# Graph attention on TensorE: four rows at a time instead of two, with three banks for transposed rows and one for the v product

## The chip, the cores and the metric

The kernel runs on one core of a Trainium2 chip. The metric is the device time of one execution in microseconds (us).

## What is computed

Four layers work on the same 512 nodes with 512 features and on 8704 edges, each with a residual and a layer norm around it: dense attention with a bias made of the edges (layer 0), a graph convolution (1), a relational convolution with a two-layer product behind it (2), and attention along the edges with a two-layer product (3). The change touches the two attentions alone. Layer 0, cut to it:

```python
bias = full((n, n), NEG); bias[diag, diag] = 0.0; bias[dst, src] = edge_weight
q, k, v = split(x @ Wqkv.T + bqkv, 3)            # 8 heads of 64 features
scores = einsum('hnd,hmd->hnm', q, k) / sqrt(64) + bias
attn = softmax(scores, axis=-1)
out = einsum('hnm,hmd->hnd', attn, v)            # then out @ Wo.T + bo
h = layer_norm(x + attn_out, g1, beta1)
```

Layer 3 has the same sum over the edges of a node, which the kernel also computes densely: the bias is then the logarithm of how often an edge occurs, and the rows with no edge are set to zero by a factor (`deg`).

## The kernel before

Everything is written for one core with a program of its own for each engine. The order on each engine is written out by hand, and semaphores carry what one needs of another: `full[b]` and `free[b]` count the uses of PSUM bank b. `psum_plan` gives each tile its bank and its number among the bank's uses; `begin(name)` on TensorE waits until the use before it was freed, `finish` says that the tile is full, `frees` that it was read.

The program runs: counts of the edges (two sweeps), q, k and v of layer 0, attention 0, output projection, layers 1 and 2, v, q and k of layer 3, attention 3 (so called after its layer), output projection, and the last product.

An attention has 32 **rows** (the code's items m): a row is one block of 128 nodes of one head, against all 512. Eight rows in a row belong to one pair of heads p, four blocks i times two heads e. Each row goes through the engines like this:

- TensorE, L600: the **scores**, a 128x512 tile in bank m % 4. Three products (the high and low halves of q and k) of 64 partitions each; the two heads of a pair stand on different halves of the partitions, so two rows are computed side by side.
- VectorE, L1272 (`peak_of`): scale, bias and row maximum in one instruction, out of the bank into `sp` (a ring of six, two of whose tiles are called `rel_rows` and `deg_rows`). This frees the bank.
- ScalarE, L830: the exponent, with its sum. VectorE, L1279: the sum's reciprocal. POOL, L381 (`scale_rows`): the row is scaled; after every third row POOL also makes the low half of a later weight piece (L367).
- TensorE, L609: four **transposes** into one bank for `probT`, 4 + m % 2. ScalarE (L838, even rows) or VectorE (L1295, odd rows) copies them to `probT` in SBUF, which has room for four heads.
- TensorE, L625: the **v product** of a pair of heads into one bank (6 + p % 2), in four **quarters** j, each of two instructions with two passes. When it is complete, ScalarE (L800) writes its high half to `th` and VectorE (L1048) its low half to `tl` and frees the bank; this pair of copies is `mixed`.

On TensorE a step q is: scores of rows 2q and 2q + 1, transposes of rows 2q - 4 and 2q - 3, and from step 6 on one quarter. The last pair's four quarters come in one step at the end. In attention 0 VectorE also has `call_sum(0)` (L1247 to L1252), which sums four planes of edge counts for the next layer; it comes behind the copies of the last rows and ahead of the low halves of the third and fourth pair. TensorE's program behind attention 0 is the output projection, whose first instruction is L478 (attention 3: L507).

```python
for t in (2 * q - 4, 2 * q - 3):
    if 0 <= t < ITEMS:
        pe.wait_ge(s["scaled"], base + t + 1)
        begin(("probT", a, t))
```

Of the kernel before, what the change touches and what calls it, by code (L numbers as in the profile page):

```python
# [26 lines left out]
P = 128  # L27
# [37 lines left out]
def psum_plan():  # L65
# [7 lines left out]
    def attention(a):  # L73
        for m in range(ITEMS):
            use(("score", a, m), m % 4)
            use(("probT", a, m), 4 + m % 2)
        for p in range(HEADS // 2):
            use(("mix", a, p), 6 + p % 2)
# [41 lines left out]
PAIR = 2 * T  # L120

# [12 lines left out]
def build(nc, x0, x0t, edges, edge_rows, edge_w, weights, rows_of, cols_of, rel_b, ident_d, iota_d, later_d, out):  # L134
# [5 lines left out]
    with ExitStack() as ctx:  # L140
# [119 lines left out]
        def ps(name):  # L260
            return bank[PLAN[name][0]]
# [202 lines left out]
        def _(pe):  # L464
# [123 lines left out]
            def attention(a, base):  # L588
# [3 lines left out]
                for q in range(ITEMS // 2 + 5):  # L592
                    if q < ITEMS // 2:
# [10 lines left out]
                    for t in (2 * q - 4, 2 * q - 3):  # L604
# [6 lines left out]
                    last = HEADS // 2 - 1  # L611
                    quarters = [(p, j) for p in range(last) for j in range(T) if q == 4 * p + 6 + j]
                    if q == 4 * last + 6:
                        quarters = [(last, j) for j in range(T)]
                    for p, j in quarters:
                        name = ("mix", a, p)
                        if j == 0:
                            wait_freed(pe, ("probT", a, PAIR * p + PAIR - 2))
                            wait_freed(pe, ("probT", a, PAIR * p + PAIR - 1))
# [171 lines left out]
        def _(act):  # L791
# [33 lines left out]
            def attention(a, base):  # L825
                for m in range(ITEMS + 4):
                    if m < ITEMS:
                        wait_freed(act, ("score", a, m))
                        c = base + m
                        act.activation(sp[m % SP][:], sp[m % SP][:], ACT.Exp, bias=peak[:, c:c + 1], scale=-1.0,  # L830
                                       accum_out=total[:, c:c + 1]).then_inc(s["exped"], 1)
                    t = m - 4
                    if t >= 0 and t % 2 == 0:
                        p, i, e, hd = item(t)
                        if hd >= 4:
                            wait_full(act, ("mix", a, p - 2))
                        wait_full(act, ("probT", a, t))
                        frees(act.copy(probT[:, hd % 4, :, i * P:(i + 1) * P],  # L838
                                       ps(("probT", a, t))[:].rearrange("p (j n) -> p j n", j=T)), ("probT", a, t))
                    if m >= 20 and (m - 20) % PAIR == 0:  # L840
                        mixed(a, (m - 20) // PAIR)
# [757 lines left out]
```

## Time and profile before

| what | us |
|---|---|
| median of 3 runs | 569.53 (568.75 to 570.74) |
| the profiled execution's own time | 569.0 |
| its span | 566.1 |
| TensorE busy | 524.4 |
| VectorE busy | 395.6 |
| POOL busy | 268.2 |
| ScalarE busy | 225.9 |

The span is from the first to the last instruction on the core; the 2.9 us between it and the execution's own time lie around the program. In the profile PE is TensorE, PEld its weight loads, DVE VectorE, ACT ScalarE, SP SyncE; L12 is line 12 of the kernel. The ends of matmuls are modelled, so their starts are the better measure. A float32 transpose or quarter shows as one instruction for each pass.

### The profile page before, as it was taken

How to read it: one execution, taken by the hardware profiler on the slowest of the kernel's cores; microseconds unless marked ns; L12 is line 12 of the kernel's file. 1: busy time of each engine (PE TensorE's matmuls, PEld its weight loads, DVE VectorE, ACT ScalarE, POOL GpSimd, SP SyncE). 2: the span in 40 equal slices, each digit the busy share in tenths (PEclk: the TensorE clock that was granted, in tenths of full speed). 3: DMA queues.
4: the chain of work that ended last, by engine and by line, in shares of the span. 5: the costliest groups of instructions: out<-in, count | busy, mean ns of one | idle time of the engine just before them, and what ended most of it. 6: DMA issues, size and time to landing. Idle time of an engine off the chain costs nothing.

```text
span 566.1 us, 7808 instructions
## 1 busy us (share of the span) xinstructions
PE 524.4 (93%) x2540; PEld 348.7 (62%) x2540; DVE 395.6 (70%) x946; ACT 225.9 (40%) x473; POOL 268.2 (47%) x258
## 2 busy tenths in 40 slices
PE   7399999999998999998999999998999998999881
PEld 2144444444875554776777888887877885554760
DVE  6988898999986777766666863546327635774647
ACT  2030080003526665557441233234624225765435
POOL 5546645667828776003540561443242653766000
PEclk9699999999999999999999999999999999999997
DMA  6950000000177220233653553212462853100001
GB/s 207 379 205 0 2 0 1 0 0 2 38 260 231 67 56 19 47 122 113 187 149 109 150 167 105 100 41 72 125 178 70 259 169 83 48 2 1 0 0 75
DMA packets 30169, 54.37 MB, mean 96 GB/s; under 512 B 4962, under 2 KB 6446, under 8 KB 29624
## 3 DMA queue, kind: packets, MB, share of 16 engines
q1 hardware_dynamic: 17212, 29.50, 17.1%
q0 software_dynamic: 11696, 18.91, 11.5%
q10 hardware_dynamic: 1228, 5.54, 2.6%
q8 instruction: 17, 0.28, 0.2%
q14 instruction: 16, 0.13, 0.1%
HBM read 51.78 MB, written 2.17 MB: 95 GB/s over the span
## 4 chain that ended last, share of the span: by engine, by line
PE 72%; DVE 9%; POOL 5%; DMA 5%; ACT 4%; issue 4%; SPq 0%; DVEq 0%; POOLq 0%; ACTq 0%
PE bank L530 18%; PE bank L507 10%; PE bank L509 9%; PE bank L508 9%; PE bank L625 5%; PE bank L609 4%; PE bank L600 3%; PE bank L702 3%; PE bank L704 3%; PE bank L703 3%; POOL edge_bias L409 2%; POOL wl L367 2%; DVE ewn L1160 2%; DMA wraw<-w_o 1%; PE bank L577 1%
## 5 line engine op out<-in xcount | busy, mean ns | idle before, releaser
L367 POOL TENSOR_TENSOR wl<-wraw,wh 128x512 fp32r<-128x512 f32 (+1 forms) x78 | 104.1, 1352 | 94.1 <-DMA wh<-w 15.4
L530 PE MATMUL bank<-hot 128*128 128x512 bf16 x544 | 119.6, 383 | 10.5 <-DVE hot L1136 10.5
L530 PEld LDWEIGHTS bank<-hot 128*128 128x128 bf16 x544 | 53.4, 99 | 76.7 <-DVE hot L1136 11.9
L409 POOL DMA_INDIRECT edge_bias<-ewn,cell_at x68 | 76.5, 1125 | 45.0 <-DVE cell_at L1130 24.3
L507 PE MATMUL bank<-wh,tl 128*128 128x512 f32 x176 | 70.9, 403 | 1.1 <-POOL wl L367 1.0
L509 PE MATMUL bank<-wh,th 128*128 128x512 f32 x176 | 68.8, 391 | 0.0
L508 PE MATMUL bank<-wl,th 128*128 128x512 f32 x176 | 68.8, 391 | 0.0
L830 ACT ACTIVATE sp<-sp,peak 128x512 f32<-128x512 f32 x44 | 31.8, 722 | 24.8 <-DVE peak L1272 24.4
L1136 DVE TENSOR_SCALAR hot<-iota,pair_dst,digit 128x1024 bf16<-128x1024 f16 x68 | 41.0, 602 | 0.0
L1118 DVE SCALAR_TENSOR_TENSOR eq<-keyb,key,later 128x384 f16<-128x384 f16 (+1 forms) x68 | 40.7, 623 | 0.0
L507 PEld LDWEIGHTS bank<-wh,tl 128*128 128x128 f32 x176 | 33.0, 188 | 12.3 <-issue 4.2
L1272 DVE CUSTOM_DVE_ANT_0 sp<-bank,nbias 128x512 f32<-128x512 f32 x44 | 29.8, 684 | 11.2 <-PE bank L600 11.2
L509 PEld LDWEIGHTS bank<-wh,th 128*128 128x128 f32 x176 | 33.0, 188 | 7.2
L508 PEld LDWEIGHTS bank<-wl,th 128*128 128x128 f32 x176 | 33.1, 188 | 6.3
L1135 DVE TENSOR_SCALAR hot<-iota,ef 128x512 bf16<-128x512 f16 x68 | 26.7, 392 | 12.9 <-PE bank L530 11.3
L625 PE MATMUL bank<-probT,v 128*64 128x512 f32 x128 | 33.0, 612 | 0.0
L1048 DVE TENSOR_TENSOR tl<-bank,th 128x512 fp32r<-128x512 f32 x32 | 21.9, 687 | 15.5 <-ACT th L805 9.8
L507 PE MATMUL bank<-th,wl 128*128 128x512 f32 x80 | 31.2, 390 | 0.9 <-issue 0.9
L508 PE MATMUL bank<-tl,wh 128*128 128x512 f32 x80 | 31.1, 389 | 0.0
L509 PE MATMUL bank<-th,wh 128*128 128x512 f32 x80 | 31.1, 389 | 0.0
L815 ACT ACTIVATE gap<-h,neg 128x512 f32<-128x512 f32 x24 | 17.4, 725 | 28.3 <-DVE neg L1059 28.3
L800 ACT CAST msgh<-bank 128x512 fp32r<-128x512 f32 x16 | 9.4, 588 | 42.9 <-DVE bank L1372 42.9
(202 smaller groups left out, 1072.3 us busy)
## 6 DMA issues: line engine op xcount, KB each, us to landing
wraw<-w SPq DMA_DIRECT2D x26, 256.0 KB, 2.7
wh<-w POOLq DMA_DIRECT2D x6, 1024.0 KB, 6.0
keyb<-edge_keys ACTq DMA_DIRECT2D x4, 1088.0 KB, 11.9
wh<-w_rel POOLq DMA_DIRECT2D x4, 1024.0 KB, 6.3
wraw<-w_rel SPq DMA_DIRECT2D x16, 256.0 KB, 2.8
wraw<-w_qkv SPq DMA_DIRECT2D x8, 256.0 KB, 6.3
wh<-w_o POOLq DMA_DIRECT2D x2, 1024.0 KB, 5.9
wraw<-w_o SPq DMA_DIRECT2D x8, 256.0 KB, 3.7
```

The costliest lines, as they stand in the source:

```text
L367: pool.tensor_tensor(wl[n % WSLOTS][:, k, 0:width], wraw[:, q % 3, 0:width], wh[n % WSLOTS][:, k, 0:width], ALU.subtract).then_inc(s["w_lo ...
L409: pool.indirect_dma_start(out=bias_dram, out_offset=bass.IndirectOffsetOnAxis(ap=cell_at[:, c:c + 1], axis=0), in_=ewn[:, c:c + 1], in_off ...
L507: pe.matmul(ps(name)[:], al, bh, start=start and k == 0, stop=False)
L508: pe.matmul(ps(name)[:], ah, bl, start=False, stop=False)
L509: mm = pe.matmul(ps(name)[:], ah, bh, start=False, stop=stop and k == ks - 1)
L530: mm = pe.matmul(ps(name)[:], hot[:, slot, 0, i * P:(i + 1) * P], hot[:, slot, 1 + kind, :], start=False, stop=last, skip_group_check=True)
L625: mm = pe.matmul(ps(name)[HD * e:HD * e + HD, :], v[:, j, hd * HD:(hd + 1) * HD], probT[:, hd % 4, j, :], start=j == 0, stop=j == T - 1, s ...
L830: act.activation(sp[m % SP][:], sp[m % SP][:], ACT.Exp, bias=peak[:, c:c + 1], scale=-1.0, accum_out=total[:, c:c + 1]).then_inc(s["exped" ...
L1118: return dve.scalar_tensor_tensor(out=eq[:, k, :], in0=keyb[:, bass.ds(c * P, WINDOW * P)], scalar=key[:, bass.ds(c, 1)], in1=later[:], op ...
L1135: dve.tensor_scalar(hot[:, slot, 0, :], iota[:, 0:N], ef[:, 0, bass.ds(j, 1)], None, ALU.is_equal)
L1136: dve.tensor_scalar(hot[:, slot, 1:3, :].rearrange("p a n -> p (a n)"), iota[:], pair_dst[:, bass.ds(j, 1)], digit[:, bass.ds(j, 1)], ALU. ...
L1272: frees(dve.tensor_tensor_reduce(sp[m % SP][:], ps(name)[:], nbias[:, item(m)[1], :], -HD ** -0.5, 3e38, ALU.add, ALU.min, peak[:, c:c + 1 ...
```

## The change

One step of TensorE is now a **batch** b of four rows: scores of rows 4b to 4b + 3, transposes of rows 4b - 4 to 4b - 1, and from batch 3 on two quarters. Transposed rows go round three banks (4, 5, 6), and all four v products use bank 7. ScalarE and VectorE get orders to match: copies of transposed rows lie between exponents and between peaks, and `mixed` of the first two pairs stands at the start of batches 5 and 7. `call_sum(0)` stays where it was.

```diff
--- before.py
+++ after.py
@@ -73,9 +73,9 @@
     def attention(a):
         for m in range(ITEMS):
             use(("score", a, m), m % 4)
-            use(("probT", a, m), 4 + m % 2)
+            use(("probT", a, m), 4 + m % 3)
         for p in range(HEADS // 2):
-            use(("mix", a, p), 6 + p % 2)
+            use(("mix", a, p), 7)
 
     def tiles(name, first, n=4):
         for i in range(n):
@@ -118,6 +118,7 @@
 PLAN = psum_plan()
 
 PAIR = 2 * T
+BATCHES = ITEMS // 4
 
 
 def item(m):
@@ -589,8 +590,10 @@
                 q_done, k_done, v_done = 4 * (a // 3 + 1), 4 * (a // 3 + 1), 4 * (a // 3 + 1)
                 pe.wait_ge(s["q_ready"], q_done)
                 pe.wait_ge(s["k_ready"], k_done)
-                for q in range(ITEMS // 2 + 5):
-                    if q < ITEMS // 2:
+                for b in range(BATCHES + 2):
+                    for q in (2 * b, 2 * b + 1):
+                        if q >= ITEMS // 2:
+                            break
                         for part, (left, right) in enumerate(((ql, kh), (qh, kl), (qh, kh))):
                             for m in (2 * q, 2 * q + 1):
                                 p, i, e, hd = item(m)
@@ -601,22 +604,19 @@
                                                start=part == 0, stop=part == 2)
                                 if part == 2:
                                     finish(mm, ("score", a, m))
-                    for t in (2 * q - 4, 2 * q - 3):
+                    for t in range(4 * b - 4, 4 * b):
                         if 0 <= t < ITEMS:
                             pe.wait_ge(s["scaled"], base + t + 1)
                             begin(("probT", a, t))
                             for j in range(T):
                                 mm = pe.transpose(ps(("probT", a, t))[:, j * P:(j + 1) * P], sp[t % SP][:, j * P:(j + 1) * P], ident[:])
                             finish(mm, ("probT", a, t))
-                    last = HEADS // 2 - 1
-                    quarters = [(p, j) for p in range(last) for j in range(T) if q == 4 * p + 6 + j]
-                    if q == 4 * last + 6:
-                        quarters = [(last, j) for j in range(T)]
+                    quarters = [(p, j) for p in range(HEADS // 2) for j in range(T) if min(2 * p + 3 + j // 2, BATCHES + 1) == b]
                     for p, j in quarters:
                         name = ("mix", a, p)
                         if j == 0:
-                            wait_freed(pe, ("probT", a, PAIR * p + PAIR - 2))
-                            wait_freed(pe, ("probT", a, PAIR * p + PAIR - 1))
+                            for t in range(PAIR * p + PAIR - 3, PAIR * p + PAIR):
+                                wait_freed(pe, ("probT", a, t))
                             if p == 0:
                                 pe.wait_ge(s["v_ready"], v_done)
                             begin(name)
@@ -823,25 +823,38 @@
                 act.wait_ge(normed[L], i + 1)
 
             def attention(a, base):
-                for m in range(ITEMS + 4):
-                    if m < ITEMS:
-                        wait_freed(act, ("score", a, m))
-                        c = base + m
-                        act.activation(sp[m % SP][:], sp[m % SP][:], ACT.Exp, bias=peak[:, c:c + 1], scale=-1.0,
-                                       accum_out=total[:, c:c + 1]).then_inc(s["exped"], 1)
-                    t = m - 4
-                    if t >= 0 and t % 2 == 0:
-                        p, i, e, hd = item(t)
-                        if hd >= 4:
-                            wait_full(act, ("mix", a, p - 2))
-                        wait_full(act, ("probT", a, t))
-                        frees(act.copy(probT[:, hd % 4, :, i * P:(i + 1) * P],
-                                       ps(("probT", a, t))[:].rearrange("p (j n) -> p j n", j=T)), ("probT", a, t))
-                    if m >= 20 and (m - 20) % PAIR == 0:
-                        mixed(a, (m - 20) // PAIR)
-                for p in range(HEADS // 2):
-                    if PAIR * p + 20 >= ITEMS + 4:
-                        mixed(a, p)
+                def exponent(m):
+
+                    wait_freed(act, ("score", a, m))
+                    c = base + m
+                    act.activation(sp[m % SP][:], sp[m % SP][:], ACT.Exp, bias=peak[:, c:c + 1], scale=-1.0,
+                                   accum_out=total[:, c:c + 1]).then_inc(s["exped"], 1)
+
+                def even_row(t):
+
+                    p, i, e, hd = item(t)
+                    if hd >= 4:
+                        wait_full(act, ("mix", a, p - 2))
+                    wait_full(act, ("probT", a, t))
+                    frees(act.copy(probT[:, hd % 4, :, i * P:(i + 1) * P],
+                                   ps(("probT", a, t))[:].rearrange("p (j n) -> p j n", j=T)), ("probT", a, t))
+
+                for b in range(BATCHES + 1):
+                    if b >= 5 and b % 2:
+                        mixed(a, (b - 5) // 2)
+                    if b < BATCHES:
+                        exponent(4 * b)
+                    if b:
+                        even_row(4 * b - 4)
+                    if b < BATCHES:
+                        exponent(4 * b + 1)
+                    if b:
+                        even_row(4 * b - 2)
+                    if b < BATCHES:
+                        exponent(4 * b + 2)
+                        exponent(4 * b + 3)
+                for p in range(2, HEADS // 2):
+                    mixed(a, p)
 
             def mixed(a, p):
                 high(("mix", a, p), th[:, p, :], s["th_ready"])
@@ -1278,29 +1291,38 @@
                     dve.wait_ge(s["exped"], c + 1)
                     dve.reciprocal(scale[:, c:c + 1], total[:, c:c + 1]).then_inc(s["inverse"], 1)
 
-                for q in range(ITEMS // 2 + 2):
-                    if q < ITEMS // 2:
-                        peak_of(2 * q)
-                    if 1 <= q <= ITEMS // 2:
-                        inverse_of(2 * q - 2)
-                        inverse_of(2 * q - 1)
-                    if q < ITEMS // 2:
-                        peak_of(2 * q + 1)
-                    t = 2 * q - 3
-                    if t >= 0:
-                        p, i, e, hd = item(t)
-                        if hd >= 4:
-                            wait_full(dve, ("mix", a, p - 2))
-                        wait_full(dve, ("probT", a, t))
-                        frees(dve.tensor_copy(probT[:, hd % 4, :, i * P:(i + 1) * P],
-                                              ps(("probT", a, t))[:].rearrange("p (j n) -> p j n", j=T)), ("probT", a, t))
-                    if q >= 11 and (q - 11) % T == 0:
-                        mixed(a, (q - 11) // T)
+                def odd_row(t):
+
+                    p, i, e, hd = item(t)
+                    if hd >= 4:
+                        wait_full(dve, ("mix", a, p - 2))
+                    wait_full(dve, ("probT", a, t))
+                    frees(dve.tensor_copy(probT[:, hd % 4, :, i * P:(i + 1) * P],
+                                          ps(("probT", a, t))[:].rearrange("p (j n) -> p j n", j=T)), ("probT", a, t))
+
+                for b in range(BATCHES + 1):
+                    if b:
+                        inverse_of(4 * b - 1)
+                    if b < BATCHES:
+                        peak_of(4 * b)
+                        if b >= 5 and b % 2:
+                            mixed(a, (b - 5) // 2)
+                        peak_of(4 * b + 1)
+                    if b:
+                        odd_row(4 * b - 3)
+                    if b < BATCHES:
+                        inverse_of(4 * b)
+                        peak_of(4 * b + 2)
+                        inverse_of(4 * b + 1)
+                    if b:
+                        odd_row(4 * b - 1)
+                    if b < BATCHES:
+                        peak_of(4 * b + 3)
+                        inverse_of(4 * b + 2)
                 if a == 0:
                     call_sum(0)
-                for p in range(HEADS // 2):
-                    if T * p + 11 > ITEMS // 2 + 1:
-                        mixed(a, p)
+                for p in range(2, HEADS // 2):
+                    mixed(a, p)
 
             def mixed(a, p):
                 base = 0 if a == 0 else 24
```

The end of attention 0 on TensorE before, from the last transposed rows on (`free4` and so on are the waits for bank 4; L625 are the quarters, the last row is the output projection):

```order
L625 MATMUL bank<-probT,v 64x512 x2
L609 MATMUL bank<-ident,sp 128x128 [waits free4,scaled]
L609 MATMUL bank<-ident,sp 128x128 x3
L609 MATMUL bank<-ident,sp 128x128 [waits free5,scaled]
L609 MATMUL bank<-ident,sp 128x128 x3
L625 MATMUL bank<-probT,v 64x512 x2
L625 MATMUL bank<-probT,v 64x512 [waits free7,free5,free4]
L625 MATMUL bank<-probT,v 64x512 x7
L478 MATMUL bank<-add,ones 128x512 [waits free0,w_low,add2_ready]
```

The same place in the changed kernel:

```order
L612 MATMUL bank<-ident,sp 128x128 [waits free4,scaled]
L612 MATMUL bank<-ident,sp 128x128 x3
L612 MATMUL bank<-ident,sp 128x128 [waits free5,scaled]
L612 MATMUL bank<-ident,sp 128x128 x3
L625 MATMUL bank<-probT,v 64x512 x4
L625 MATMUL bank<-probT,v 64x512 [waits free5,free7,free4,free6]
L625 MATMUL bank<-probT,v 64x512 x7
L479 MATMUL bank<-add,ones 128x512 [waits free0,w_low,add2_ready]
```

Two quarters of the third pair now come after the last transposes instead of one, and the `free7` of the last pair stands for the use of bank 7 by the third pair, which before was in bank 6.

VectorE in the changed kernel over the same stretch (L1300 copies a transposed row, L1260 to L1265 are `call_sum`, L1061 the low halves of the third and fourth pair):

```order
L1300 COPY probT<-bank 128x4x128 [waits full4,full7]
L1285 ISA sp,peak<-bank,nbias 128x512 [waits full5,full3]
L1285 ISA peak 128x1
L1292 RECIPROCAL scale<-total 128x1 [waits exped] x2
L1300 COPY probT<-bank 128x4x128 [waits full6,full7]
...
L1260 TENSOR_TENSOR call_a<-counts 128x1024
L1261 TENSOR_TENSOR call_a<-call_a,counts 128x1024 [waits dve_chain]
L1262 TENSOR_TENSOR call_a<-call_a,counts 128x1024 [waits dve_chain]
L1265 TENSOR_TENSOR call_a<-call_a,ident 128x128 [waits dve_chain]
L1061 TENSOR_TENSOR tl<-bank,th 128x512 [waits th_ready] x2
```

The last five operations stand in the same order as before; what is new is that TensorE's last quarters wait for the first of the two in the last row.

## Rows read from the trace of the kernel before

**Rows 1.** The page: busy time of each engine, and the chain that ended last.

```profile
PE 524.4 (93%) x2540; PEld 348.7 (62%) x2540; DVE 395.6 (70%) x946; ACT 225.9 (40%) x473; POOL 268.2 (47%) x258
...
PE 72%; DVE 9%; POOL 5%; DMA 5%; ACT 4%; issue 4%; SPq 0%; DVEq 0%; POOLq 0%; ACTq 0%
```

**Rows 2.** Windows: length, busy us of PE, PEld, DVE, ACT, POOL, clock, DMA.

```profile
172.90:187.80 14.90, 12.46 (x83) 8.04 (x82) 12.76 (x44) 11.34 (x29) 12.48 (x17) 1.00 0.76 227
187.80:219.00 31.20, 30.92 (x189) 15.94 (x188) 21.56 (x71) 21.41 (x54) 23.22 (x29) 1.00 0.18 52
```

**Rows 3.** Timeline of TensorE in attention 0, middle: start, length, operation.

```profile
189.73 0.66 PE L609 MATMUL bank<-ident,rel_rows 128*128 128x128 f32 x4
...
190.75 1.08 PE L625 MATMUL bank<-probT,v 128*64 128x512 f32 x4
191.76 0.50 PE L600 MATMUL bank<-kh,ql 64*128 64x512 f32 x2
...
192.66 1.09 PE L609 MATMUL bank<-ident,sp 128*128 128x128 f32 x8
```

**Rows 4.** Timeline of VectorE and ScalarE, the same stretch.

```profile
193.38 0.22 DVE L1279 RECIPROCAL scale<-total 128x1 f32<-128x1 f32 x2
193.49 0.72 ACT L830 ACTIVATE rel_rows<-rel_rows,peak 128x512 f32<-128x512 f32 x1 [0.92 <-DVE peak L1272]
...
194.12 0.18 ACT L830 ACTIVATION_READ_ACCUMULATOR rel_rows<-rel_rows,peak 128x1 f32 x1
194.22 0.56 ACT L838 COPY probT<-bank 128x512 f32<-128x512 f32 x1
```

**Rows 5.** Timeline, start of attention 0: first scores, peaks, transposes, first quarter.

```profile
172.89 0.50 PE L600 MATMUL bank<-kh,ql 64*128 64x512 f32 x2
...
173.69 0.55 PE L600 MATMUL bank<-kh,ql 64*128 64x512 f32 x2
...
174.01 0.69 DVE L1272 CUSTOM_DVE_ANT_0 sp<-bank,nbias 128x512 f32<-128x512 f32 x1 [0.32 <-PE bank L600]
...
187.83 1.08 PE L625 MATMUL bank<-probT,v 128*64 128x512 f32 x4
```

**Rows 6.** Timeline, end of attention 0, TensorE and VectorE.

```profile
218.99 4.62 PE L625 MATMUL bank<-probT,v 128*64 128x512 f32 x20
219.17 0.69 DVE L1295 COPY probT<-bank 128x512 f32<-128x512 f32 x1 [1.34 <-PE bank L609]
219.78 1.20 DVE L1247 TENSOR_TENSOR call_a<-counts 128x1024 int16<-128x1024 int16 x1
...
223.54 0.50 PE L478 MATMUL bank<-add,ones 2*128 2x512 f32 x1
...
224.77 1.28 DVE L1048 TENSOR_TENSOR tl<-bank,th 128x512 fp32r<-128x512 f32 x2
```

**Rows 7.** Timeline of TensorE, attention 3: first scores, and the projection's first matmul.

```profile
473.22 0.50 PE L600 MATMUL bank<-kh,ql 64*128 64x512 f32 x2 [1.50 <-issue]
...
523.02 0.50 PE L507 MATMUL bank<-wh,tl 128*128 128x512 f32 x1
```

**Rows 8.** TensorE around its idle stretches: timeline, then windows (busy us, instructions, granted clock).

```profile
23.24 1.03 PE L530 MATMUL bank<-hot 128*128 128x512 bf16 x2 [9.28 <-DVE hot L1136]
...
554.18 0.40 PE L509 MATMUL bank<-wh,hidh 128*128 128x512 f32 x1
...
16.00:21.00 5.00, 0.00 (x0) 0.54 0.91 378
...
26.00:31.00 5.00, 5.00 (x23) 0.94 1.01 406
...
556.00:561.00 5.00, 0.00 (x0) 0.81 0.18 69
```

**Rows 9.** Longest waits of TensorE, 223 to 300, then 300 to 400 us: total, times, longest.

```profile
PE bank L671 <- DVE rowl L1346: 2.0, 3, 1.0
...
PE bank L493 <- DVE tl L1048: 1.6, 1, 1.6
```

## The prediction

> **What bounds the kernel now.** I read the page first. TensorE is busy for 93% of the span and carries 72% of the chain that ended last [rows 1], so a microsecond of TensorE delay is a microsecond of kernel unless a later stage absorbs it. Next I read the windows over the two attention stages, the only code the diff touches [rows 2]. Each has three parts. In the start (172.9 to 187.8) TensorE is busy 12.46 of 14.90 us: the ring score, peak, exponent, scale, transpose is being filled. In the middle (187.8 to 219.0) it is busy 30.92 of 31.20 us. In the end it runs quarters of the v product alone. The second attention has the same shape.
>
> Then the timeline of TensorE [rows 3]. One step of the old order is two transposed rows, one quarter and two scores. Transposes begin at 189.73 and again at 192.66, so a step is 2.93 us and four rows 5.86. The transposes take 1.02 of it (to 190.75), the quarter 1.01 (to 191.76), the scores 0.90. Where the kind of work changes the first matmul costs more: the scores of rows 0 and 1 are followed by those of rows 2 and 3 after 0.80 us instead of 0.90 [rows 5]; a row's four transposes last 0.66 and eight last 1.09, so four more inside a run cost 0.43; five quarters in a row take 4.55 us, from 218.99 to 223.54 [rows 6], so each after the first costs (4.55 - 1.01) / 4 = 0.89.
>
> **What the change removes.** No matmul, copy, exponent or DMA goes or comes; only order and banks change. A batch of four rows has one run of each kind where there were two. That saves 0.10 on scores, about 0.15 on transposes (2.04 becomes 1.02 + 2 x 0.43) and 0.12 on quarters: 0.37 us a batch, so the batch takes 0.80 + 0.90 + 1.88 + 1.90 = 5.5 us instead of 5.86. Five batches with quarters save 1.8 us in each attention. The first batches have no quarters, and there TensorE isn't what sets the pace.
>
> **What it adds, one: a ring of 5.2 us a batch.** With three banks for four transposed rows, the fourth row of a batch waits until ScalarE has copied out the first one, and ScalarE does that copy behind the exponent of the next batch's first row. That exponent hangs on VectorE, and this on the fourth row of the batch before. I add the ring up from one fourth row to the next: its transposes 0.66 [rows 3]; VectorE's copy of it 0.61, to the start of the next operation [rows 6]; the peak of the last score 0.69 [rows 5]; its exponent with the sum 0.81; the reciprocal 0.11; the next peak 0.69; the next exponent up to the copy 0.73; ScalarE's copy 0.56 [rows 4]. That is 4.86, and eight handovers at the 0.03 to 0.06 seen between these rows make it 5.2. It is shorter than 5.5, so it hides in the batches with quarters, and longer than the 3.6 us of work in those without.
>
> **The layout of one attention**, from its first score matmul. Old order in the trace [rows 5, 6]: first quarter at 187.83 - 172.89 = 14.9, transposes done at 218.99 - 172.89 = 46.1, end at 223.54 - 172.89 = 50.7. New order: row 3 is transposed at about 7.25. (Rows 4 to 7 must be scored first, and row 7 waits for the peak of row 3. The first peak starts at 174.01; three more, with two reciprocals between them that wait for the exponents, put the end of the fourth at 4.2, the end of row 7's scores at 5.1. Rows 0 to 2 are transposed from 5.1; row 3 waits for the copy of row 0, which stands behind the exponent of row 4.) Two turns of the ring later, at 17.65, row 11 is transposed and at 18.2 the first quarter starts. That is 3.3 later than before, with the work of four more rows done. Four batches at 5.55 (5.5 and a few hundredths of waiting at the fourth row) lead to 40.5. Two quarters, 1.9, and the last four rows, 2.6 with 0.7 of waiting for copies that no scores cover any more, lead to 45.2. **So up to here 0.9 us are won, while one quarter has been put off**: six remain instead of five. The faster batches are nearly eaten by the ring at the start.
>
> **What it adds, two: the bank of the v product.** All four head pairs now use bank 7. The last pair's first quarter waits until VectorE has taken the third pair's low part out of it; before, it waited for the second pair's, long gone. In attention 0 VectorE's program has the sum of the counts ahead of that low part, as the order printed ahead shows. It starts at 219.78 and the low parts at 224.77, so 4.99 us stand ahead [rows 6]. New order: last transposes 45.2, copy of row 31 until 45.9, sum until 50.9, low part 0.65 more, so TensorE may go on at about 51.6. Its two quarters of the third pair were through at 47.1. **It stands for about 4.5 us**, then takes 3.6 for the last four quarters: end at 55.2 instead of 50.7, **4.5 us later**. Queued behind that wait are the output projection and all after it. VectorE's own delay (the last low part now comes after the last quarters, the two low parts of the counts behind it) is as long and lies beside it. POOL's weights and residual are done sooner than needed; their DMAs wait for buffers, not for TensorE's last quarters, and cost nothing.
>
> In attention 3 there is no such sum. The order is the same, from 473.22 to 523.02 in the trace, 49.8 us [rows 7] (its start is faster, since the weight pieces that POOL takes between its scale operations are half as wide there). The new layout is bound by the ring, which has no POOL in it, so it gives 45.2 again. Two quarters end at 47.2, ScalarE's high part, 0.6 like its other copies, and VectorE's low part, 0.65, follow with handovers, TensorE goes on at 48.6 after 1.5 us, and ends at 52.2: **2.4 us later**.
>
> **TensorE's clock.** This trace shows it twice after idleness [rows 8]. TensorE's matmuls end at 13.96, and the mean of 0.54 for 16 to 21 says that the granted clock was at half (1.2 GHz) from about 16.4. Work came back at 23.24 and the clock at 26.6 (0.94 over 26 to 31 is 0.6 us of half), after 3.4 us at half speed. At the end the last matmul ends at 554.6 and the clock falls near 559.1 (0.81 over 556 to 561), 4.5 us later. In between, with no gap over 1.6 us, it stays at 1.00. A gap of some 4 us lies between the falls after 2.4 and after 4.5. Both ends: no fall costs 0, a fall costs half of the 3.4 us until the clock is back, 1.7. I take the fall: the gap at 13.96 also had matmuls without a pause ahead of it, and there it took only 2.4.
> The Trainium skill ("TensorE: Matmul & The Clock Gate", Why this matters for your kernels) also has idle gaps of a few microseconds between bursts throw the engine back to half rate; by that rule the sum is the 577.6 below, without it 575.9.
>
> **Sum.** 4.5 + 2.4 + 1.7 = 8.6 on the profiled execution's 569.0 gives **577.6 us**. That execution is 0.5 below the median of the three runs, 569.53, and inside their spread.
> Between the attentions TensorE's waits are for VectorE and ScalarE, at most 2.0 us in one group from 223 to 300 and 1.6 us from 300 to 400 [rows 9]. Those work on what TensorE hands them and come later with it; no wait there is for POOL or a DMA, which could have stood still meanwhile. So nothing absorbs the delay.
>
> **Rivals.**
> *The clock holds* (chance 0.24). All else as above: 575.9. The fall at the end, after 4.5 us, speaks for it. Still slower.
> *The wait for the bank is covered* (0.04). This is also the case that the order isn't what I read. Then both attentions end as the layout says without the wait: 45.2 + 1.9 + 3.6 = 50.7 against 50.7, and 50.7 against 49.8: 570, no change. For it: nothing; the order shows the sum of the counts ahead of the low part.
> *TensorE alone sets the pace* (0.04). If ScalarE's copy of a batch's first row is done before the fourth row's transposes are due, the ring doesn't close. Then two starts of 5.2 become 3.6 (3.2 saved), and the waits at row 3 and at the last rows go (about 1.4): 4.6 in each attention, 577.6 - 9.2 = 568.4, and with the clock holding 566.7, faster. It decides at 1.3 us after the batch's first transpose; the copy needs its exponent to end by then, and that hangs on a peak that the fourth row before holds up.
> *The ring closes in the full batches too* (0.06). A few handovers of 0.1 instead of 0.04 bring it from 5.2 to over 5.5; at 5.8 all ten full batches cost 0.3 more: 580.6.
> The forecast itself has 0.62.
>
> **How the numbers follow.** A measurement of this kernel can tell about 0.3%, 1.7 us, from no change. The forecast, the clock that holds and the longer ring are slower: 0.92. The covered bank is within: 0.04. TensorE alone: 0.04 faster. The range runs from 1.9 below the clock that holds, 574.0, for errors of the layout (on the old order it comes within 0.2 us of the trace in each attention), to 580.6, the longer ring; beyond both ends lies about 0.15 to 0.2.
>
> **What would show it.** Right: attention 0 lasts 55 us and attention 3 52, first score to first matmul of the output projection; TensorE idle 4 to 5 us before the last pair's quarters in attention 0, 1.5 in attention 3, released by VectorE's low part; granted clock under 1.00 around 220 to 230; waits of 0.7 to 0.8 at the fourth row and at the scores of rows 7, 11 and 15; batches of 5.5 in the middle. Wrong: a middle batch of 5.8 or more, no gap in attention 0, or a later stage that is shorter than before.

## The result and the profile after

| | before | changed |
|---|---|---|
| median of the runs, us | 569.47 (568.75 to 570.74, 4 runs) | 577.66 (576.59 to 578.23, 4 runs) |
| the profiled execution, us | 569.0 | 577.45 |
| its span, us | 566.1 | 575.4 |

The changed kernel takes 1.0143 times as long, interval 1.0123 to 1.0163: slower by 8.2 us. The forecast was 577.6.

The page answers to [rows 1]: no engine's busy time rose by as much as 1% (the weight loads beside TensorE's matmuls by just 1%), TensorE's busy share fell, and VectorE's share of the chain rose from 9% to 11%. The third row is new in the waits: the v product, released by VectorE's low part.

```profile
PE 524.7 (91%) x2525; PEld 352.3 (61%) x2540; DVE 398.2 (69%) x946; ACT 227.0 (39%) x473; POOL 269.0 (47%) x258
...
PE 70%; DVE 11%; DMA 5%; ACT 5%; POOL 4%; issue 4%; SPq 0%; DVEq 0%; POOLq 0%; ACTq 0%
...
L625 PE MATMUL bank<-probT,v 128*64 128x512 f32 x128 | 31.9, 626 | 6.6 <-DVE tl L1061 6.6
```

The windows over attention 0, with the columns of [rows 2]: start, middle, and the end from 219.00 on, just after the third pair's last two quarters began.

```profile
173.80:192.10 18.30, 15.52 (x97) 9.93 (x96) 14.55 (x49) 13.05 (x34) 15.22 (x19) 1.00 0.62 188
192.10:219.00 26.90, 26.51 (x171) 15.38 (x172) 20.15 (x66) 20.43 (x50) 20.11 (x26) 1.00 0.20 58
219.00:230.60 11.60, 6.55 (x24) 1.84 (x20) 6.46 (x7) 0.59 (x1) 4.88 (x4) 0.85 0.00 0
```

The start is 3.4 longer, the middle 4.3 shorter, and the end, which was 4.55 us of quarters, is 11.6 us long. The timeline of TensorE shows the pieces (start, length, operation, idle time before it and its releaser): the first scores, the wait at the fourth row, one that has POOL in it, one batch of the middle (from score to score), the third and fourth row of another, and the end.

```profile
173.80 0.50 PE L603 MATMUL bank<-kh,ql 64*128 64x512 f32 x2
...
181.07 0.63 PE L612 MATMUL bank<-ident,sp 128*128 128x128 f32 x4 [0.64 <-ACT probT L839]
...
191.54 0.66 PE L612 MATMUL bank<-ident,deg_rows 128*128 128x128 f32 x4 [0.70 <-POOL deg_rows L382]
192.12 1.94 PE L625 MATMUL bank<-probT,v 128*64 128x512 f32 x8
193.99 0.50 PE L603 MATMUL bank<-kh,ql 64*128 64x512 f32 x2
...
199.59 0.50 PE L603 MATMUL bank<-kh,ql 64*128 64x512 f32 x2
...
207.72 0.60 PE L612 MATMUL bank<-ident,rel_rows 128*128 128x128 f32 x4
208.37 0.63 PE L612 MATMUL bank<-ident,deg_rows 128*128 128x128 f32 x4
...
218.72 1.94 PE L625 MATMUL bank<-probT,v 128*64 128x512 f32 x8
...
225.71 5.00 PE L625 MATMUL bank<-probT,v 128*64 128x512 f32 x16 [5.05 <-DVE tl L1061]
230.63 0.50 PE L479 MATMUL bank<-add,ones 2*128 2x512 f32 x1
```

POOL in that start, ahead of the scale of row 5: a weight piece that waited for its DMA:

```profile
183.03 1.28 POOL L368 TENSOR_TENSOR wl<-wraw,wh 128x512 fp32r<-128x512 f32 x1 [1.36 <-DMA wh<-w]
```

VectorE beside the end, the counterpart of [rows 6]: the sum of the counts, which starts behind its last transposed row, and only then the low part that frees bank 7.

```profile
219.51 1.58 DVE L1260 TENSOR_TENSOR call_a<-counts 128x1024 int16<-128x1024 int16 x1
...
220.71 0.59 ACT L800 CAST th<-bank 128x512 fp32r<-128x512 f32 x1 [2.11 <-PE bank L625]
...
224.47 0.49 DVE L1265 TENSOR_TENSOR call_a<-call_a,ident 128x128 int16<-128x128 int16 x2
224.88 0.69 DVE L1061 TENSOR_TENSOR tl<-bank,th 128x512 fp32r<-128x512 f32 x1
```

ScalarE has the high part written at 221.3; the low part could follow at once, and starts at 224.88. The clock meanwhile, in windows of TensorE (length, busy us, instructions, granted clock, DMA):

```profile
221.00:226.00 5.00, 0.29 (x2) 0.90 0.00 0
226.00:231.00 5.00, 5.00 (x17) 0.75 0.00 0
```

0.90 over 5 us is 1.0 us at half speed (1.2 GHz), 0.75 is 2.5: the clock was low from about 225.0 to 228.5. The sixteen passes of the last quarters took 4.92 us, from 225.71 to 230.63.

Attention 3, the counterpart of [rows 7]: three fourth rows 5.13 apart, the last of all transposed rows, the wait of 1.50 before the last pair, and the projection.

```profile
480.48 0.50 PE L603 MATMUL bank<-kh,ql 64*128 64x512 f32 x2 [1.51 <-issue]
...
487.71 0.63 PE L612 MATMUL bank<-ident,sp 128*128 128x128 f32 x4 [0.63 <-ACT probT L839]
...
492.84 0.63 PE L612 MATMUL bank<-ident,sp 128*128 128x128 f32 x4 [0.69 <-ACT probT L839]
...
497.97 0.63 PE L612 MATMUL bank<-ident,deg_rows 128*128 128x128 f32 x4 [0.70 <-ACT probT L839]
...
524.62 0.66 PE L612 MATMUL bank<-ident,sp 128*128 128x128 f32 x4 [0.29 <-POOL sp L382]
...
528.65 3.65 PE L625 MATMUL bank<-probT,v 128*64 128x512 f32 x16 [1.50 <-DVE tl L1061]
532.23 0.50 PE L508 MATMUL bank<-wh,tl 128*128 128x512 f32 x1
```

So attention 0 lasts 56.83 us, first score to first matmul of the projection (50.65 before), and attention 3 lasts 51.75 (49.80). These 6.2 and 1.95 are the 8.2 between the medians. The spans lie 9.3 apart; 0.9 of that is ahead of attention 0, in code that is the same, and its start moves from 172.99 to 174.34 between the profiles of the kernels below. Between the attentions 249.85 us pass, 0.2 more than before, so nothing was absorbed there.

All experiments start from the changed kernel. "Length" below is measured as here.

### The profile page after: what moved, and what is told of

It is laid out like the page before. It is cut to its first block, busy times and chain, and to the rows that moved or that the text cites. A ratio compares the mean times of both kernels' runs of the same rounds, so it can differ in the third digit from the quotient of the medians.

```text
span 575.4 us, 7799 instructions
## 1 busy us (share of the span) xinstructions
PE 524.7 (91%) x2525; PEld 352.3 (61%) x2540; DVE 398.2 (69%) x946; ACT 227.0 (39%) x473; POOL 269.0 (47%) x258
## 4 chain that ended last, share of the span: by engine, by line
PE 70%; DVE 11%; DMA 5%; ACT 5%; POOL 4%; issue 4%; SPq 0%; DVEq 0%; POOLq 0%; ACTq 0%
PE bank L531 18%; PE bank L508 10%; PE bank L510 9%; PE bank L509 9%; PE bank L625 4%; PE bank L612 3%; PE bank L702 3%; PE bank L704 3%; PE bank L703 3%; PE bank L603 2%; POOL edge_bias L410 2%; DVE ewn L1173 2%; DMA wraw<-w_o 1%; PE bank L578 1%; DMA wh<-w 1%
## 5 line engine op out<-in xcount | busy, mean ns | idle before, releaser
L410 POOL DMA_INDIRECT edge_bias<-ewn,cell_at x68 | 77.7, 1142 | 43.9 <-DVE cell_at L1143 25.4
L1061 DVE TENSOR_TENSOR tl<-bank,th 128x512 fp32r<-128x512 f32 x32 | 22.0, 688 | 23.8 <-ACT th L800 13.7
L625 PE MATMUL bank<-probT,v 128*64 128x512 f32 x128 | 31.9, 626 | 6.6 <-DVE tl L1061 6.6
L612 PE MATMUL bank<-ident,sp 128*128 128x128 f32 x176 | 24.8, 278 | 2.8 <-ACT probT L839 2.0
```

The costliest lines, as they stand in the source:

```text
L410: pool.indirect_dma_start(out=bias_dram, out_offset=bass.IndirectOffsetOnAxis(ap=cell_at[:, c:c + 1], axis=0), in_=ewn[:, c:c + 1], in_off ...
L612: mm = pe.transpose(ps(("probT", a, t))[:, j * P:(j + 1) * P], sp[t % SP][:, j * P:(j + 1) * P], ident[:])
L625: mm = pe.matmul(ps(name)[HD * e:HD * e + HD, :], v[:, j, hd * HD:(hd + 1) * HD], probT[:, hd % 4, j, :], start=j == 0, stop=j == T - 1, s ...
```

## Experiments: the wait before the last pair

**e1_sum_behind.** The sum of the counts steps behind the low part of the third pair. The shared bank stays.

```diff
+                mixed(a, 2)
                 if a == 0:
                     call_sum(0)
-                for p in range(2, HEADS // 2):
-                    mixed(a, p)
+                mixed(a, 3)
```

> The changed kernel with one thing moved: on VectorE the sum of the counts (4.99 us) goes behind the third pair's low part instead of ahead of it. Theory of the prediction: TensorE's wait in attention 0 falls from 5.05 us to about 1.5, as in attention 3, that is 3.5 us less, of which 0.4 may come back through the last low part; with so short a gap the granted clock stays at full, 1.4 us more: 577.7 - 4.7 = about 573. Rival, the clock has nothing to do with it: about 574.5, and the clock still falls near 225. Rival, the batches themselves cost and VectorE's work only moves its wait to the next stage: not below 576.5.

Measured: 571.69 (5 runs), 1.0048 of the kernel before, interval 1.003 to 1.0066. Timeline of POOL, VectorE and TensorE at the end of attention 0:

```profile
217.49 4.94 POOL L391 TENSOR_TENSOR y<-x,par 128x512 f32<-128x512 f32 x4
...
220.77 0.69 DVE L1061 TENSOR_TENSOR tl<-bank,th 128x512 fp32r<-128x512 f32 x1 [1.74 <-ACT th L800]
221.38 1.61 DVE L1260 TENSOR_TENSOR call_a<-counts 128x1024 int16<-128x1024 int16 x1
...
223.02 0.69 DVE L1261 TENSOR_TENSOR call_a<-call_a,counts 128x1024 int16<-128x1024 int16 x1
223.74 0.69 DVE L1262 TENSOR_TENSOR call_a<-call_a,counts 128x1024 int16<-128x1024 int16 x1
...
221.61 3.65 PE L625 MATMUL bank<-probT,v 128*64 128x512 f32 x16 [1.50 <-DVE tl L1061]
...
225.19 0.50 PE L479 MATMUL bank<-add,ones 2*128 2x512 f32 x1
```

The wait is 1.50 instead of 5.05, as in attention 3, where there never was a sum. The quarters take 3.58 instead of 4.92 at a granted clock of 1.00. Attention 0 is 51.68 long: one line moved on VectorE brings 5.15 of the 6.2 us back. That is 3.55 of waiting, 1.34 of clock, and 0.2 of the start, which had no wait for POOL in this execution. The median fell by 6.0 where 4.7 was expected; the expectation had 3.5 for the wait, less 0.4 that did not come back, and 1.4 for the clock, and attention 0 also began 0.3 sooner here. The rivals are out: the clock did not fall, and the time is below 574.5. Attention 3, which the edit doesn't touch, stays at 51.76.

**e2_busy_gap** keeps the wait and keeps TensorE busy in it. In attention 0 eighteen products of q and k are added ahead of the last pair, written to bank 0, which the output projection overwrites.

```diff
+                            if a == 0 and p == 3:
+                                begin(("o0", 0))
+                                for n in range(18):
+                                    pe.matmul(ps(("o0", 0))[:], qh[:, 0, 0:P], kh[:, 0, :], start=True, stop=True)
```

> The changed kernel with 18 extra matmuls of 0.22 us (4 us of TensorE work) in the gap ahead of the last pair's quarters of attention 0, into a bank that is free; their results are overwritten. The wait for the bank stays, only TensorE is no longer idle in it. Theory: the clock holds, the four quarters take 3.6 us instead of 4.9, the time falls by 1.4 us to 576.3. Rival, a fall of the clock that costs nothing, since VectorE sets the pace behind: 577.7. Rival, the extra matmuls delay the quarters: above 577.7.

Measured: 575.91 (4 runs), 1.0126, interval 1.0104 to 1.0149. Timeline and then windows of TensorE:

```profile
219.93 4.38 PE L625 MATMUL bank<-kh,qh 128*128 128x512 f32 x18
225.02 3.65 PE L629 MATMUL bank<-probT,v 128*64 128x512 f32 x16 [0.71 <-DVE tl L1065]
228.60 0.50 PE L479 MATMUL bank<-add,ones 2*128 2x512 f32 x1
...
226.00:231.00 5.00, 5.00 (x24) 1.00 0.00 0
```

The quarters start when they did (51.6 us after the first score; 51.9 in the changed kernel, whose start was 0.2 longer), but at full clock, and take 3.58. So the wait costs 3.55 by itself (5.05 less 1.50) and the clock 1.34 on top. The intervals of the ratios of the changed kernel and of this one overlap; the quarters' length in the trace is the evidence, the 1.75 us between the medians only agree with it.

**e8_half_gap** is the same edit with `range(9)`, for an idle stretch of a length in between.

> As e2, with 9 extra matmuls instead of 18: 2 us of work, then about 2.9 us without any ahead of the last pair's quarters of attention 0. Theory that every gap of a few microseconds brings the clock down: the quarters take 4.9 us or more again and the time is that of the changed kernel, 577.7. Rival, a gap of this length is short enough: quarters 3.6 us, 576 as in e2. The first fall that a profile showed came 2.4 us after the last matmul, the wait of 1.5 us in attention 3 never brought one; 2.9 lies between the two kinds, so I put it at even odds.

Measured: 577.28 (575.99 to 578.14, 4 runs), 1.0137, interval 1.0096 to 1.0177. Timeline and a window of TensorE:

```profile
225.93 3.65 PE L629 MATMUL bank<-probT,v 128*64 128x512 f32 x16 [2.70 <-DVE tl L1065]
...
226.00:231.00 5.00, 5.00 (x22) 1.00 0.00 0
```

In the profiled execution 2.70 us idle brought no fall. The other runs reach up to what a fall would give, and no profile of them exists. The profiled execution takes 0.9 more than that of e2 because attention 0 starts at 174.34 instead of 173.42, and not by its quarters. Whether the clock fell in some of the other runs stays open: this run tells the two apart only for the execution that was profiled.

## Experiments: the banks and the ring

**e3_two_v_banks** gives the third bank back: two banks for transposed rows, two for the v product, with the order of the change.

```diff
-            use(("probT", a, m), 4 + m % 3)
+            use(("probT", a, m), 4 + m % 2)
...
-            use(("mix", a, p), 7)
+            use(("mix", a, p), 6 + p % 2)
```

> The new order with the old banks: two for transposed rows, two for the v product. Theory, by the same layout: no wait ahead of the last pair's quarters in either attention, but the third row of each batch now waits for the copy of the first (about 1.2 us in the first batches, 0.6 in the middle ones), so a middle batch takes 5.9 us and each attention 53.4: 569.5 + 2.7 + 3.6 = 575.8. Rival, the single bank for the v product is the whole cost and the batches gain: 566.5.

Measured: 575.54 (4 runs), 1.0109, interval 1.0081 to 1.0137. The waits of TensorE in attention 0 (total, times, longest), and one batch of the middle:

```profile
PE bank L612 <- ACT probT L839: 5.3, 7, 1.1
```

```profile
194.27 0.50 PE L603 MATMUL bank<-kh,ql 64*128 64x512 f32 x2
...
197.42 1.06 PE L612 MATMUL bank<-ident,sp 128*128 128x128 f32 x8 [0.48 <-ACT probT L839]
...
200.28 0.50 PE L603 MATMUL bank<-kh,ql 64*128 64x512 f32 x2
```

Both attentions last 53.4, as expected. The wait for bank 7 is gone, and the third row of each batch now waits for ScalarE: a batch takes 6.01, longer than the 5.86 of four rows in the old order. So the two halves of the change belong together: a run of four transposes over two banks is worse than two runs of two. Against the changed kernel this gains in attention 0 (56.83 to 53.4) and loses in attention 3 (51.75 to 53.4). The bank trade alone is worth 1.6 us where no sum stands in the way.

**e5_copy_first** aims at the ring. ScalarE's copy of a batch's first row goes ahead of the exponent of the next one.

```diff
+                    if b:
+                        even_row(4 * b - 4)
                     if b < BATCHES:
                         exponent(4 * b)
-                    if b:
-                        even_row(4 * b - 4)
```

> The changed kernel with one swap on ScalarE: the copy of a batch's first transposed row ahead of the exponent of the next batch's first row. Theory of the ring: its path through that exponent is cut, but the exponent now waits for the transposes, and the fourth score waits longer in its place; by the layout the first batches get only 0.2 to 0.7 us shorter in each attention: about 577. Rival, the wait at the fourth row is the whole loss of the start (0.7 us in each of three batches) and goes without a price: 577.7 - 4.2 = 573.5.

Measured: 576.14 (7 runs), 1.0109, interval 1.0075 to 1.0143. The first quarter of attention 3 comes after 17.28 instead of 18.05, so 0.8 is won in three turns. The waits of TensorE in attention 3 tell why not more:

```profile
PE bank L603 <- DVE peak L1285: 1.9, 4, 0.8
```

That was 0.9 in the changed kernel. The later exponent delays what hangs on it, and the ring seems to close over the peaks. Attention 3 is 50.94 long, 0.8 shorter. Attention 0 is 57.20, longer by 0.4, though its first quarter too comes 0.6 sooner. The time is nearer to the 577 expected than to the rival's 573.5. Timeline and windows of TensorE:

```profile
225.29 5.95 PE L625 MATMUL bank<-probT,v 128*64 128x512 f32 x16 [5.05 <-DVE tl L1061]
231.18 0.50 PE L479 MATMUL bank<-add,ones 2*128 2x512 f32 x1
...
221.00:226.00 5.00, 0.71 (x2) 0.71 0.00 0
226.00:231.00 5.00, 5.00 (x16) 0.60 0.00 0
```

The same idle stretch of 5.05 us, and 2.9 + 4.0 us at half speed instead of 3.5: the quarters take 5.89.

**e6_pairs_at_start** does the first twelve rows in the old steps of two and goes over to batches at row 12, with ScalarE and VectorE to match (core of the edit, TensorE):

```diff
-                for b in range(BATCHES + 2):
+                for q in range(6):
+                    scores((q,))
+                    turned_rows((2 * q - 4, 2 * q - 3))
+                for b in range(3, BATCHES + 2):
```

> The changed kernel with the first twelve scored and eight transposed rows in steps of two, as before the change, on all engines; batches of four from the first quarter on. Banks, sum of the counts and end as in the change. Theory: the start no longer goes at the ring's 5.2 us a batch; by the layout attention 0 gets 0.8 us shorter and attention 3 1.5: 575.4. Rival, the ring at the start costs nothing against the old steps: 577.7.

Measured: 576.27 (574.33 to 578.05, 9 runs), 1.0107, interval 1.0079 to 1.0136. First quarter of attention 3 after 16.67, transposes done at 43.3 instead of 44.7, length 50.36. Attention 0 is 55.82. Its end again has a fall, here 1.9 + 1.5 us long:

```profile
224.47 5.16 PE L636 MATMUL bank<-probT,v 128*64 128x512 f32 x16 [5.05 <-DVE tl L1076]
229.56 0.49 PE L479 MATMUL bank<-add,ones 2*128 2x512 f32 x1
...
221.00:226.00 5.00, 1.53 (x4) 0.81 0.00 0
226.00:231.00 5.00, 5.00 (x19) 0.85 0.00 0
```

Starting in pairs is worth 1.4 us in attention 3 and 1.0 in attention 0 (1.5 and 0.8 were expected), the latter although its quarters took 0.17 more at the low clock. The edit takes away the ring and the longer first batches together; how much of the 1.4 is the ring alone is not shown.

## Experiments: a version that keeps the batches

**e4_quarters_first** leaves banks and sum and moves the third pair's last two quarters ahead of the last four transposes, with `mixed(a, 2)` early on ScalarE and VectorE (core, TensorE):

```diff
+                    for part in ((quarters_of, rows_turned) if b == BATCHES else (rows_turned, quarters_of)):
+                        part(b)
```

> The changed kernel with, in both attentions, the third pair's last two quarters ahead of the last four transposed rows, its high and low part taken out ahead of those rows' copies, and the sum of the counts behind that low part. Theory: nothing waits for bank 7 any more, 0.9 us stay for the copy of the last row; each attention takes 50.7: 569.5 + 0.0 + 0.9 = 570.4. Rival, the loss is in the batches and not in the bank's wait: above 574.

Measured: 570.24 (10 runs), 1.0016, interval 1.0003 to 1.0029. Timeline of TensorE at the end of attention 0:

```profile
220.30 3.65 PE L630 MATMUL bank<-probT,v 128*64 128x512 f32 x16 [1.05 <-DVE probT L1309]
```

By the interval it is still slower than the kernel before, by about 0.8 us. The copies out of bank 7 now lie beside the last transposes. What is left is 1.05 us for the copy of row 31. Both attentions last 50.8: even in attention 0, and 1.0 behind the old order in attention 3.

**e7_pairs_and_quarters_first** is e6's start with e4's end.

> The start of e6 and the end of e4 together: steps of two until the first quarter, batches of four in the middle, the third pair's quarters ahead of the last transposed rows, the sum of the counts behind its low part. Theory: what is left is the gain of the middle, 0.37 us a batch: by the layout 49.9 us for attention 0 and 49.2 for attention 3, against 50.65 and 49.8 before the change: 568.2. Rival, the batches gain nothing even in the middle: 570 or more.

Measured: 567.78 (566.05 to 571.01, 12 runs) beside 569.61 (25 runs) of the kernel before: 0.9965, interval 0.9939 to 0.9992. It beats both kernels, by 1.8 us with an interval that ends near zero. Attention 3 is 49.37, 0.4 shorter than before. Attention 0 is 50.72 in the profile, no shorter. VectorE at its start tells why:

```profile
173.68 1.53 DVE L1295 TENSOR_TENSOR v<-bank,par 128x512 f32<-128x512 f32 x2 [0.15 <-DVE v L1295]
175.49 0.69 DVE L1308 CUSTOM_DVE_ANT_0 sp<-bank,nbias 128x512 f32<-128x512 f32 x1 [0.27 <-DVE v L1295]
```

In this execution VectorE still had two copies of v to make when the first scores were done, and its first peak came 2.10 us after the first score (at 173.39). Before it was 1.12 [rows 5]. In e6, whose start has the same order, it was 1.12 too, and the first quarter came 17.17 after the first score; here it came after 18.03. So this start cost about 0.9, and without it attention 0 would be 49.9, as expected. That the other executions had no such start is inferred, no profile of them exists. The two profiled executions have equal spans (566.1 before, 566.2 here), so the gain of 1.8 stands on the medians alone.

## Why the prediction was right

The time, 577.66 for 577.6, and the steps:

- **The batch.** 5.5, or 5.55 with the wait at the fourth row, was forecast; it measured 5.60 (193.99 to 199.59). Its scores took 1.60 (forecast 1.70), its transposes 2.13 (195.59 to 197.72; forecast 1.88), its quarters 1.87 (1.90), so the transposes are the term that was too small. The fourth row starts 0.65 after the third (207.72 to 208.37) instead of 0.43, and 0.14 after ScalarE's copy of the batch's first row has ended (at 208.23). So a wait of about 0.2 for that copy is left in the full batches, where a few hundredths were forecast. A batch saves 0.26 of 5.86, where the term was 0.37 with no wait in it. Direction right, size two thirds.
- **The ring.** 5.2 forecast, 5.13 measured in attention 3, with waits of 0.63 to 0.70 for ScalarE's copy. Row 3 came 7.27 after the first score (forecast 7.25), the first quarter 18.3 and 18.05 (18.2). Adding the ring up out of single rows and handovers worked. The waits at the scores of rows 7, 11 and 15 were 0.2 to 0.3, not the 0.7 to 0.8 that was named as a sign.
- **POOL in the ring** was not forecast. In attention 0 of this profile two rows wait for POOL's scale, the longer time 0.70 (the row at 191.54), and the first quarter is 0.3 later than in attention 3. It belongs to this execution and not to the order: POOL's weight piece at 183.03, ahead of the first of these scales, had waited for its DMA and began 9.2 us after the first score. In e1, e2, e4 and e8, whose start has the same order, it began after 7.8 to 8.5, no row of the start waits for POOL, and the first quarter comes after 18.1.
- **Transposes done** at 45.2 forecast, 44.9 and 44.7 measured (the starts of the quarters behind them). The faster batches were eaten by the start, as the layout said: 1.2 and 0.5 us are left of them, with one quarter put off. The layout's own terms, 40.5 and 1.9 and 2.6, add up to 45.0; the 45.2 is 0.2 more than they give.
- **The bank of the v product, attention 0.** The gap of 5.05 is released by the low part, with all four planes of the sum ahead of it, as the order of VectorE said it would be. TensorE went on at 51.9 (forecast 51.6): the sum took 5.37 us (219.51 to 224.88) where the layout had the 4.99 of [rows 6]; the whole difference is its first operation, 1.58 instead of 1.20. Without the clock's share, attention 0 is 4.85 longer (4.5 forecast). e1 shows the cause: with the sum behind the low part the wait is 1.50.
- **Attention 3.** 1.50 us of waiting as forecast, length 51.75 instead of 52.2: 1.95 longer than before instead of 2.4. Of the 0.45 too much, 0.2 is the adding named above, and about 0.2 lies in the last four rows: they took 2.41 instead of 2.6, and the one wait there is the 0.29 for POOL at 524.62, not 0.7 for ScalarE's copies.
- **The clock.** The fall came, between the two ends: 4.4 us after the last matmul's end at 220.66, beside 2.4 and 4.5 in [rows 8]. It cost 1.34, the forecast was 1.7. The term took half of the 3.4 us that the clock stayed low in [rows 8] after work came back. Here that was 2.8 us (225.71 to 228.5), half of it 1.4. The same works for e5 (4.7 us, 2.3 lost) and e6 (3.0 us, 1.5 lost), so this time differs from profile to profile, and the forecast could not know which one it would meet.
The Trainium skill ("TensorE: Matmul & The Clock Gate", Why this matters for your kernels) has idle gaps of a few microseconds throw the engine back; the trace agrees for all three profiles with a gap of 5.05, and the 2.70 of e8 brought no fall.
- **Nothing absorbs it.** The same groups of waits stand behind attention 0 as in [rows 9], and the stretch between the attentions kept its length.

The mechanism was right in each large term, and the closeness of the number was in part luck. The misses are 0.35 too little and 0.45 too much for the two attentions, and 0.35 too much for the clock. They cancel in part: the three terms measured 8.15 for 8.6. The 0.45 that is left is hidden by the base, the profiled execution's 569.0, which lies 0.5 below the median of the runs; that is how the median came within 0.1 us. A fall like that of e5 would have added 1 us.

The rivals: the clock that holds is refuted in this profile, the covered bank by the wait of 5.05, TensorE alone by the waits at the fourth row. The ring that closes in the full batches too, at 5.8 a batch, is refuted by the 5.60, though a wait of 0.2 is left there.

## What to carry to other kernels

When buffers are traded between two uses, ask for the one that loses a buffer where the instruction that frees it stands in its engine's queue. One unrelated sum of 5 us ahead of it cost more than all the faster batches gave; its move alone brought 5 us back.

Longer runs of one kind saved a tenth of a microsecond per change of kind, but they lengthened the pipeline's start and put work off to its end. Short steps at the start, long ones in the middle and the buffer's last use pulled forward at the end shed most of the price: e7 came out 1.8 us ahead of the kernel before, with an interval from 0.5 to 3.5.

## What the runs showed of the hardware

- **The same idle stretch, different falls.** Three profiles had TensorE idle for 5.05 us at the same place. The clock fell about 4.4 (changed kernel), 2.9 (e5) and 4.7 us (e6) after the last matmul and stayed at half for about 3.5, 6.9 and 3.4 us; the quarters behind it took 4.92, 5.89 and 5.09 us instead of 3.58. An edit can look up to 1 us worse (e5, attention 0) through this alone. Stretches of 2.70 (e8), 1.50 (e1), 1.05 (e4) and 0.71 us (e2) ahead of the same quarters showed no fall in their profiles.
- **POOL beside VectorE doubles the time of the sum.** In e1 POOL's four operations of L391 end at 222.43. The operation of the sum that starts before that takes 1.61, the two that start behind it 0.69 each. In the changed kernel L391 runs until 223.9, and all three operations of the sum over the planes take about 1.6. e4 shows the same border: L391 ends at 222.5, the operation that starts at 221.39 takes 1.64, the one at 223.06 takes 0.69. The first one, beside POOL in all profiles, varies from 1.1 (e3) to 1.6. So of the 5.37 us that stood ahead of the low part, about 2.7 (three operations, 0.9 each) come from POOL's work beside it. That is an estimate from the rows of e1; no kernel without that work of POOL's was run. The Trainium skill ("SBUF — State Buffer", Who interferes with whom) has a VectorE instruction with two inputs in SBUF contend with a GpSimd instruction that reads SBUF; these rows agree.
- **A start varies by a microsecond.** Code that no edit touches put the start of attention 0 between 172.99 and 174.34 us in the profiles of the changed kernels, and VectorE's first peak came 1.12 us behind the first score in all profiles but that of e7, where it was 2.10. The next weight piece of POOL, which waits for a DMA, began 7.8 (e2) to 9.2 us (changed kernel) after the first score.
